# Layer 0's edge loop: one tile in eight takes its pre-activation rows from DRAM by two indirect transfers

## The reference, cut to what matters

```python
x1 = x[edges[0]]
x2 = x[edges[1]]
e = jnp.concatenate([x1, x2], axis=1) @ Ww + bw        # 12288 x 1024
e = e.reshape(-1, H, 2 * HD).transpose(1, 0, 2)        # 8 heads of 128
e = jax.nn.leaky_relu(e, 0.01)
w = (e @ Wa + ba)[..., 0]
mat = jnp.full((H, n, n), -jnp.inf, jnp.float32)
mat = mat.at[:, edges[0], edges[1]].set(w)
mat = jax.nn.softmax(mat, axis=-1)
```

## Time and profile before

| | |
|---|---|
| three runs | 1785.69, 1786.20, 1795.17 us (median 1786.2) |
| the profiled execution | 1774.8 us, span 1773.1 us |
| mean granted TensorE clock | 0.974 of full speed |
| PE busy over the span | 1651.2 us (93%) |
| first L1372 of the loop to the last | 112.4 to 407.3 us |

### The profile page before, as it was taken

The page is one execution under the profiler, slowest core; times in us unless marked ns, Lnnn a source line. Parts: engine busy times, 40 slices in busy tenths (PEclk is TensorE's granted clock), DMA queues, the critical chain, the costliest instruction groups (busy, mean ns, idle before and its releaser), DMA issues.

```text
span 1773.1 us, 23528 instructions
## 1 busy us (share of the span) xinstructions
PE 1651.2 (93%) x7277; PEld 934.7 (53%) x7307; DVE 884.8 (50%) x2162; ACT 500.7 (28%) x1586; POOL 647.0 (36%) x756
## 2 busy tenths in 40 slices
PE   6989999999898999999999998697899999999898
PEld 4634444445755646555556666442444555555555
DVE  8878887878835453344354157785523101111322
ACT  1124444447431413223231125110200111111234
POOL 5868788773232333333441814566200000000000
PEclk9999999999899999999998998899899999999999
DMA  8030101105413223222316744455326121310020
GB/s 317 1 104 25 60 25 30 50 14 133 128 48 129 78 82 91 58 82 64 83 38 139 267 146 144 136 149 162 105 72 218 61 88 47 101 62 22 6 67 18
DMA packets 119614, 161.76 MB, mean 91 GB/s; under 512 B 49497, under 2 KB 61721, under 8 KB 119154
## 3 DMA queue, kind: packets, MB, share of 16 engines
q1 hardware_dynamic: 93056, 115.43, 20.9%
q0 software_dynamic: 18592, 29.91, 6.3%
q10 hardware_dynamic: 7890, 15.44, 2.6%
HBM read 145.26 MB, written 15.47 MB: 91 GB/s over the span
## 4 chain that ended last, share of the span: by engine, by line
PE 81%; DVE 8%; DMA 4%; issue 3%; POOL 2%; ACT 2%; ACTq 0%; another core or an unknown queue 0%; DVEq 0%; POOLq 0%; SPq 0%
PE psum L374 79%; DMA arena<-tab_h,sd_t 1%; POOL ring L631 1%; DVE stats L471 1%; DMA ring<-tab_h,sd_t 1%; DVE ring L1306 1%; DVE xn L2074 0%; PE psum L1034 0%; DVE xn L2080 0%; DMA xT<-tab_h,sd_t 0%; POOL arena L631 0%; DVE xn L2093 0%; ACT xT L415 0%; DMA x<-in_x 0%; PE psum L405 0%
## 5 line engine op out<-in xcount | busy, mean ns | idle before, releaser
L374 PE MATMUL psum<-arena 128*128 128x384 f32 (+9 forms) x1804 | 313.8, 328 | 18.8 <-DVE arena L670 5.6
L374 PE MATMUL psum<-arena,ring 128*128 (+1 forms) x1478 | 321.2, 362 | 9.6 <-issue 6.2
L374 PE MATMUL psum<-xT,ring 128*128 128x384 f32 x928 | 308.7, 493 | 7.9 <-ACT xT L415 4.2
L374 PE MATMUL psum<-ring,arena 128*128 128x512 f32 (+1 forms) x570 | 263.0, 608 | 11.2 <-DVE ring L670 6.6
L374 PEld LDWEIGHTS psum<-arena 128*128 128x128 f32 (+5 forms) x1804 | 193.1, 152 | 148.0 <-issue 74.5
L374 PE MATMUL psum<-ring,xT 128*128 128x512 f32 x552 | 249.8, 605 | 1.3 <-issue 0.7
L374 PEld LDWEIGHTS psum<-xT,ring 128*128 128x128 f32 x928 | 177.0, 192 | 133.1 <-issue 16.3
L374 PEld LDWEIGHTS psum<-arena,ring 128*128 128x128 bf16 (+1 forms) x1504 | 137.5, 113 | 130.4 <-issue 29.3
L1085 ACT ACTIVATE ring<-ring 128x128 f32<-128x128 f32 x416 | 123.3, 297 | 173.3 <-DVE ring L1372 173.3
L374 PEld LDWEIGHTS psum<-ring,arena 128*128 128x128 f32 (+1 forms) x570 | 99.9, 188 | 134.9 <-issue 133.9
L374 PEld LDWEIGHTS psum<-ring,xT 128*128 128x128 f32 x552 | 104.3, 194 | 122.2 <-issue 119.3
(11 more groups left out here) (481 smaller groups left out, 1739.4 us busy)
## 6 DMA issues: line engine op xcount, KB each, us to landing
ring<-in_L_ffn_w SPq DMA_DIRECT2D x22, 1024.0 KB, 7.3
ring<-in_L_gnn_m_w SPq DMA_DIRECT2D x8, 1024.0 KB, 5.8
ring<-in_L_ffn_expert_weights SPq DMA_DIRECT2D x8, 1024.0 KB, 5.7
ring<-tab_key ACTq DMA_DIRECT2D x24, 256.0 KB, 3.1
ring<-in_L_gnn_Wv SPq DMA_DIRECT2D x5, 1024.0 KB, 5.1
tab_w<-xn SPq DMA_DIRECT2D x6, 768.0 KB, 14.9
ring<-in_L_gnn_Ww SPq DMA_DIRECT2D x4, 1024.0 KB, 17.3
ring<-in_L_gnn_wq SPq DMA_DIRECT2D x4, 1024.0 KB, 5.5
```

The costliest lines, as they stand in the source:

```text
L374: return nc.tensor.matmul(o, a, b, start=start, stop=stop)
```

## The change

Tile 7 of every turn (`BROUGHT`) gets its rows another way. U and V are also stored in f32 to two DRAM tables; for each brought tile POOL issues an indirect gather of 128 rows of U (4 KB each) into `z_row`, and four tiles later a second one of V that adds to it. PE leaves out the 12 wide products of that tile but keeps its five short ones. DVE makes the `edge_is` one-hots of tiles b = 1 and b = 5 in POOL's place, and sums 3 heads instead of 4; ACT sums 5. `zeros_r` and its nine products go; six filler products stand there. SP's clearing of `tab_x` comes behind the last stores of the tables.

```diff
+        DVE_HOTS = (1, 5)
+        BROUGHT = UN - 1
+        tab_uv = [dram(f"tab_{s_}", (N, 2 * D)) for s_ in "uv"]
+        uv_row = cnt_src[:].rearrange("p c n -> p (c n)")[:, 0:2 * D].rearrange("p (b n) -> p b n", b=2)
+        z_row = ring.slot(1).rearrange("p c n -> p (c n)")[:, 2 * D:4 * D]
+        DVE_HEADS = 3
...
+            def store_unit(u):
+                r, q, t = UNITS[u]
+                sp.wait_ge(uv_made, u + 1)
+                sp.dma_start(tab_uv[r][t * P:(t + 1) * P, q * D:(q + 1) * D], uv_row[:, u % 2, :]).then_inc(uv_stored[u % 2], 16)
+
+            for u in range(len(UNITS) - 2):
+                store_unit(u)
             banks.drained(sp, "sortk")
             sp.dma_start(tab_key, key_b).then_inc(keys_stored, 16)
             sp.wait_ge(keys_stored, 16)
             for g in range(2):
                 load_keys(sp, g)
+            for u in range(len(UNITS) - 2, len(UNITS)):
+                store_unit(u)
...
-            for w in (512, 512, 512, 256, 256, 256, 128, 128, 128):
-                mm(b[:, 0:w], zeros_r[:, 0:P], zeros_r[:, 0:w], True, True)
-            keep_clock(b, 3)
+            keep_clock(b, 6)
...
-                    pe.wait_ge(z_free, T + 1)
-                    gathered(0, 0, 0)
-                    gathered(0, 0, 1)
-                    pe.wait_ge(hote_made, T + 1)
+                    if b != BROUGHT:
+                        pe.wait_ge(z_free, T + 1)
+                        gathered(0, 0, 0)
+                        gathered(0, 0, 1)
+                    if b in DVE_HOTS:
+                        pe.wait_ge(hotd_made, 2 * i + DVE_HOTS.index(b) + 1)
+                    else:
+                        pe.wait_ge(hote_made, 6 * i + b + 1 - sum(h < b for h in DVE_HOTS))
                     mm(wide[:, bass.ds(cs * 512 + cd * P + CNT0 * 512, P)], edge_is[:, j, k, 0, :], edge_is[:, j, k, 1, :], False, False)
+                    if b == BROUGHT:
+                        mm(wide[:, bass.ds(T + CNT0 * 512 + N, 1)], edge_is[:, j, k, 1, :], ones_b[:, 0:1], False, False)
+                        pe.wait_ge(eq_free, T + 1)
+                        linear(0)
+                        linear(1).then_inc(z_full, 1)
+                        mm(small[:, 0:P], node_is[:, j, k, 1, :], node_is[:, j, k, 1, :], True, True).then_inc(eq_full, 1)
+                        continue
...
             def top_part(u):
                 b = banks.filled(act, unit_name(u))
+                if u >= 2:
+                    act.wait_ge(uv_stored[u % 2], 16 * (u // 2))
+                nc.scalar.activation(uv_row[:, u % 2, :], b, ACT.Copy).then_inc(uv_made, 1)
                 nc.scalar.activation(unit_part(u, 0), b, ACT.Copy).then_inc(hi_made, 1)
...
-                    for h in range(H8 // 2, H8):
+                    for h in range(DVE_HEADS, H8):
...
+            def bring(turn, s_):
+                if s_ == 0:
+                    if turn == 0:
+                        for k in range(2):
+                            pool.wait_ge(uv_stored[k], 16 * len(UNITS) // 2)
+                        pool.wait_ge(row_at_made, 1)
+                    nc.gpsimd.indirect_dma_start(z_row, None, tab_uv[0], bass.IndirectOffsetOnAxis(
+                        ap=row_at[:, 0, turn:turn + 1].bitcast(U32), axis=0)).then_inc(u_landed, 16)
+                else:
+                    pool.wait_ge(u_landed, 16 * turn + 16)
+                    nc.gpsimd.indirect_dma_start(z_row, None, tab_uv[1], bass.IndirectOffsetOnAxis(
+                        ap=row_at[:, 1, turn:turn + 1].bitcast(U32), axis=0), compute_op=ALU.add).then_inc(v_landed, 16)
+
             for q in range(ST):
                 pool.wait_ge(w_ready, q + 1)
+                if q == 0 or (q % UN == BROUGHT and q + 1 < ST):
+                    bring((q + 1) // UN, 0)
+                if q % UN == 3:
+                    bring(q // UN, 1)
                 if q + HOT_AHEAD < ST:
                     hot_edges(q + HOT_AHEAD)
...
+            def hot_edges(T, b):
+                j, k = b // TB, b % TB
+                V.tensor_tensor(edge_is[:, j, k], iota_b[:].unsqueeze(1).broadcast_to([P, 2, P]),
+                                key_rq_b[:, bass.ds(2 * T, 2)].unsqueeze(2).broadcast_to([P, 2, P]),
+                                ALU.is_equal).then_inc(hotd_made, 1)
...
+                if b == BROUGHT:
+                    dve.wait_ge(v_landed, 16 * i + 16)
+                z_of = z_row.rearrange("p (h d) -> p h d", h=H8) if b == BROUGHT else z_bank[:, b % 2]
...
-                V.tensor_reduce(w_sum[:, b, 0:H8 // 2], prod2[:, b % 2, 0:H8 // 2, :], AX, ALU.add).then_inc(halves_summed, 1)
+                V.tensor_reduce(w_sum[:, b, 0:DVE_HEADS], prod2[:, b % 2, 0:DVE_HEADS, :], AX, ALU.add).then_inc(halves_summed, 1)
...
+                        if b in DVE_HOTS and not (last and b == DVE_HOTS[1]):
+                            hot_edges(UN * i + b + TB, (b + TB) % UN)
```

More of the change, by code:

```diff
@@ L277, in gnn_ffn_program @@
         hote_made = sem("hote_made")
+        hotd_made = sem("hotd_made")
         z_full = sem("z_full")
@@ L854, in gnn_ffn_program @@
         HOT_AHEAD = UN - 2
+        DVE_HOTS = (1, 5)
[3 more added lines that the diff above has]
+        z_row = ring.slot(1).rearrange("p c n -> p (c n)")[:, 2 * D:4 * D]
+        node_at = sb("node_at", [P, 2, ST // UN])
+        row_at = sb("row_at", [P, 2, ST // UN], I32)
+        row_at_made = sem("row_at_made")
+        uv_made = sem("uv_made")
+        uv_stored = sems("uv_stored", 2)
+        u_landed = sem("u_landed")
+        v_landed = sem("v_landed")
+        DVE_HEADS = 3
         def to_bucket(pool, q, most):
@@ L981, in linear @@
                     def linear(s_):
-                        mm(lin, node_is[:, j, k, s_, :], lin_parts[:, s_, bass.ds(ends[s_], 1), :, :].rearrange("p a k h -> p (a k h)"),
-                           s_ == 0, s_ == 1)
+                        return mm(lin, node_is[:, j, k, s_, :],
+                                  lin_parts[:, s_, bass.ds(ends[s_], 1), :, :].rearrange("p a k h -> p (a k h)"), s_ == 0, s_ == 1)
                     if k == 0:
                         pe.wait_ge(hot_made, 2 * i + j + 1)
-                    pe.wait_ge(z_free, T + 1)
-                    gathered(0, 0, 0)
-                    gathered(0, 0, 1)
-                    pe.wait_ge(hote_made, T + 1)
-                    mm(wide[:, bass.ds(cs * 512 + cd * P + CNT0 * 512, P)], edge_is[:, j, k, 0, :], edge_is[:, j, k, 1, :], False, False)
+                    if b != BROUGHT:
[6 more added lines that the diff above has]
+                        pe.wait_ge(hote_made, 6 * i + b + 1 - sum(h < b for h in DVE_HOTS))
+                    mm(wide[:, bass.ds(cs * 512 + cd * P + CNT0 * 512, P)], edge_is[:, j, k, 0, :], edge_is[:, j, k, 1, :], False, False)
+                    if b == BROUGHT:
[5 more added lines that the diff above has]
+                        continue
                     gathered(0, 0, 2)
@@ L1176, in hot_edges @@
             def hot_edges(T):
+                if T % UN in DVE_HOTS:
+                    return
                 j, k = T // TB % 2, T % TB
@@ L1281, in first_hot_edges @@
                                 key_rq_b[:, 0:2 * TB].unsqueeze(2).broadcast_to([P, 2 * TB, P]),
-                                ALU.is_equal).then_inc(hote_made, TB)
+                                ALU.is_equal).then_inc(hote_made, TB - 1)
+                V.memset(gate[:, 15, 15:16], 0.0).then_inc(hotd_made, 1)
+            def hot_edges(T, b):
[3 more added lines that the diff above has]
+                                ALU.is_equal).then_inc(hotd_made, 1)
             def tile_chunks():
@@ L1356, in _ @@
             V.memset(gate[:, 15, 11:12], 0.0).then_inc(heads_summed, 2)
+            for s_, of in enumerate((cs_q, cd_q)):
+                last = V.scalar_tensor_tensor(out=node_at[:, s_, :], in0=of.rearrange("p (i b) -> p i b", b=UN)[:, :, BROUGHT],
+                                              scalar=float(P), in1=key_rq[:, s_, :].rearrange("p (i b) -> p i b", b=UN)[:, :, BROUGHT],
+                                              op0=ALU.mult, op1=ALU.add)
+            od.link(last)
+            od.link(V.tensor_scalar(node_at[:], node_at[:], 0.0, None, ALU.max))
+            V.tensor_copy(row_at[:], node_at[:]).then_inc(row_at_made, 1)
             z_bank = psum[:, 0:4, :].rearrange("p (b q) n -> p b (q n)", b=2).rearrange("p b (h d) -> p b h d", h=H8)
@@ L1371, in one_tile @@
                 dve.wait_ge(heads_summed, T + 1)
-                V.scalar_tensor_tensor(out=prod2[:, b % 2], in0=z_bank[:, b % 2], scalar=0.0, in1=wa_all, op0=ALU.max,
+                if b == BROUGHT:
+                    dve.wait_ge(v_landed, 16 * i + 16)
+                z_of = z_row.rearrange("p (h d) -> p h d", h=H8) if b == BROUGHT else z_bank[:, b % 2]
+                V.scalar_tensor_tensor(out=prod2[:, b % 2], in0=z_of, scalar=0.0, in1=wa_all, op0=ALU.max,
```

4 lines of the change are left out of this document (1 added, 3 removed).

## The result

The changed kernel takes 1844.3 us (median of 4 runs, 1842.4 to 1848.9) against 1786.0 for the kernel before beside it: ratio 1.032, 95% interval 1.029 to 1.034. The forecast was 1799 us with a range of 1778 to 1822: slower was right, the size was not. The profiled execution spans 1841.4 us, at a mean granted clock of 0.944 (before 0.974).

A forecast was written before the change was run, and what follows sets the result against it. PE was taken to pace the loop, POOL close behind. On the profiled execution 1774.8 + 0.6 - 3.0 - 0.3 + 15.4 = 1787.5 us; +12.7 on the median 1786.2 gave 1799 us, range 1778 to 1822.

The forecast's parts named there:

- PE's tile 7: In the loop, PE stands at `eq_free` in tile 7, so a brought tile saves 0.25 us, not 2.5; -3.0 us in all.
- The rival in which the 33 us come back: PE does not stand at `eq_free` in tile 7, so the wide products' time returns whole: 1753 us; chance 0.07.
- The clock: PE's 3.1 us idle from tile 7 into the next turn lowers its clock: 1.28 us a turn, +15.4 us.
- The chance of 0.8: Weight given to each turn's PE gap lowering the clock, at 1.6 us each time.
- The rows' arrival: V rows for tile 7, issued at `w_ready` of tile 3, land in 6.0 us, fit into 7.0 and cost nothing.
- the 7.0 allowed: Longest way of the V rows, from issue to DVE's start on tile 7, said to do no harm: 7.0 us.
- POOL: POOL's loop work with two gathers added and four one-hots removed takes 22 us a turn (19.3 to 24.5), below the turn.
- Cover by working ahead: POOL works six tiles ahead in the loop, so single stalls behind the gathers are covered.
- The small parts: Outside PE's gap: an extra ACT copy before the loop +0.6 us, the end -0.3 us; one-hot shares, fillers and clears free.
- the rows come late, or POOL falls behind: Rival: V rows take 9 us, DVE is 2 us late each turn, up to +29 us, 1815 us; chance 0.13.

The follow-up runs named there:

- products kept: Changed kernel with both transfers made, but PE keeps tile 7's 12 wide products and DVE reads them without waiting for the rows: 1819.4 us, 1.018.
- products kept, no adding: Changed kernel, PE keeping tile 7's wide products, nobody waiting for the rows, V fetched by a plain overwriting gather: 1788.0 us, 1.006.
- with the gap removed: Changed kernel without row gathers, tile 7's short products put into an unused wide bank so PE need not wait for `eq_free`: 1779.0 us, 1.001.
- run without transfers: Changed kernel without the row gathers and the wait for them; DVE reads a constant, PE still omits tile 7's wide products: 1806.0 us, 1.010.
- Filling the gap: Changed kernel without row gathers, plus six wide products nobody reads ahead of PE's wait for `eq_free`: 1780.8 us, 1.002.
- filled gap with transfers kept: Changed kernel, gathers included, plus six wide products nobody reads ahead of PE's wait for `eq_free`: 1840.3 us, 1.037.
- two tables: Changed kernel with every second tile's scores scattered to a second, unread table, each scatter waiting for the one two tiles before: 1800.6 us, 1.013.
- shares alone: Changed kernel with PE's products kept and no row gathers or wait; table stores, re-shared heads and one-hots, and fillers stay: 1778.1 us, 1.000.

## Why the prediction was wrong

Scatter to scatter on GpSimd, in us: means over the loop, worked out from the start times of its timeline (intervals with more than 0.2 us of waiting for VectorE, and those of the last seven tiles, left out). A turn has four intervals of the first kind and one each of the others; "sum" is that turn.

| kernel | pair of one-hots between | V between | behind V | U between | behind U | sum | turn |
|---|---|---|---|---|---|---|---|
| before | 2.73 (x68) | | | | | 8 x 2.73 = 21.8 | 22.90 |
| changed | 3.19 (x46) | 3.72 | 4.56 | 2.71 | 3.48 | 27.2 | 26.98 |
| products kept | 2.73 (x48) | 3.65 | 4.51 | 2.64 | 3.60 | 25.3 | 24.87 |
| products kept, no adding | 2.91 (x48) | 2.96 | 3.32 | 2.65 | 3.59 | 24.2 | 23.71 |

The sum meets the turn within 0.5 us in the three kernels with transfers, which is what "GpSimd sets the pace" means. In the kernel before it stays 1.1 us below, and that much GpSimd waited for VectorE there (13.3 us in the loop, 1.0 a turn).

- **PE's tile 7**: right. It stands 1.60 us at `eq_free` and the whole gap is 3.6 us (forecast 1.6 and 3.1). The rival in which the 33 us come back is out: even with the gap removed, a turn is at best 1.5 us shorter, not 2.5.
- **The clock**: right in kind, close in size. The run without transfers has 1.35 us more a turn; forecast were 1.28 - 0.25 = 1.03. The window from 300 to 304 us of that run reads 0.59, which is 0.41 x 4 / 0.5 = 3.3 us at 1.2 GHz and 1.6 us lost; I had taken 1.6 us times 0.8. Filling the gap held the clock at 1.00 and took the loss from 1.0% to 0.2%. The chance of 0.8 was too careful: in the run without transfers the clock fell behind all 12 gaps, in the changed kernel behind 11 (at 403.75 it stayed 1.00, and fell behind TensorE's next wait, of 3.60 us). The Trainium skill (TensorE: Matmul & The Clock Gate, Part 1: The HAM clock gate) says that an idle TensorE is put back to half the clock, and these traces agree. But in the changed kernel this term is hidden behind GpSimd, as the filled gap with transfers kept shows (1.037 against 1.038 and 1.039 of its neighbours).
- **The rows' arrival**: the term of 6.0 us measured 6.0, partly by luck: of the plain gather's 4.4 us to V's 6.0 I had given 0.9 to the adding and 0.9 to ACT's key load, but V never lands in under 5.6 us, and issued two tiles earlier it takes 6.0 as well, so nearly all of it is the adding's. What failed is the premise that V is issued when `w_ready` of tile 3 comes. The whole way was GpSimd's lag of 1.1 to 8.4 us plus the landing, over the 7.0 allowed in 12 of the 13 turns; with two tables, where the lag is 0.3, it is 5.9 to 6.9 us in 11 of them.
- **POOL**: this is the step that failed. "I take 22, below the turn" had 24.5 as its upper end; measured are 27.0. Three terms of it were wrong. First, I added up busy time (8 x 1.055, 16 x 0.62, 8 x 0.17 us), and it gave 19.7; but a scatter waits for the landing of the one before, and the distance was already 2.73 us a tile on average, 21.8 a turn. The 17.5 us of waiting for landings in the earlier trace rows, 1.7 us a turn, which I left aside, are most of this difference; the room was 1.1 us, not 3.3. The earlier trace rows show the room directly: ahead of L1179 GpSimd waited 12.4 us for VectorE in these ten turns. Second, the four one-hots taken away counted -2.5 and were worth nothing, since they fill that wait (two more pairs moved to VectorE, or all pairs back on GpSimd: no change within 0.7 us a turn). Third, the two gathers cost 14.47 - 4 x 2.73 = 3.55 us a turn, of which the scatter held up behind V makes 1.8 and its issue with the adding 1.0. Moving the wait from the predecessor to the scatter two tiles before brought 1844 back to 1801, and did nothing in the kernel before, so the cause is shown, not argued.
- **Cover by working ahead**: "single stalls are covered" holds for the one-hots, which are made six tiles ahead. It does not hold for the V gather, which stands in order behind the scatters.
- **What the steps did to each other**: not in the sum. Intervals with a pair between them stay at 2.73 us with the products kept (2.91 without the adding) and grow to 3.19 in the changed kernel; 1.0 of these 1.84 us a turn are the slower GpSimd instructions described below. The rest I cannot assign. SyncE's two reads of the table, free before, lengthen turns once GpSimd has no room; of the turn of 33.4 us I cannot say how much is theirs.
- **The small parts** were right together: shares, stores and fillers cost nothing (1.000). The loop starts 0.4 us later (+0.6 forecast), but over all versions its start lies between 109.8 and 115.3 us, so that term alone is not shown.

The rival "the rows come late, or POOL falls behind" (13 in 100, 1815 us) was the case, at nearly twice its price, as it too was built on the busy time.

## What to carry to other kernels

When an engine issues transfers that each wait for the one before to land, cost the distance from start to start in the trace, not the busy time: work between two of them that fits into the wait is free, and taking it away brings nothing. Anything large put into that queue is paid twice, once for its issue and once because the small transfer behind it lands late. Read the engine that comes second as closely as the one that sets the pace: here it had 1.1 us of room a turn, so a saving of 1.5 us on TensorE came through only in part (22.76 us a turn against 22.99), and a cost of 3.6 us did.

## What the hardware showed that I had not expected

- The adding form of the indirect gather takes GpSimd 1.62 us to issue, the plain one 0.98 to 0.99, and 6.0 us to land against 4.1 to 4.4 (512 KB each).
- While VectorE's L1442 reads both operands from SBUF, a scatter that GpSimd starts beside it takes about 1.82 us instead of 1.05. In the changed kernel 12 of the 13 brought tiles show it (297.18 and 297.53 above are such a pair), and whenever the scatter starts, 0.31 to 0.63 us in, it ends 2.14 or 2.15 us after L1442's start, 0.9 us after L1442's end; where VectorE reads all tiles from PSUM (before, products kept, shares alone), no scatter up to the last L1442 takes over 1.5 us.
- The pair of one-hots behind that scatter takes 1.39 to 1.49 us instead of 1.21 in those 12 turns. L1442 is over by then; VectorE's L1329, which makes the node one-hots, runs beside it. The same is seen in the kernel before, where 8 of the 200 one-hots take 0.77 us instead of about 0.61, each beside L1276.
- Two scatters with nothing between them start 2.93 us apart, since GpSimd stands until the first has landed. With 1.21 us of one-hots between them it is 2.48.
